# A hybrid attention and mixture-of-experts kernel: numbering of the routing tables on ScalarE, residual sums among the row gathers, and the split of the norm's rows

## The chip, the cores and the metric

The kernel runs on one core of one Trainium2 chip. The metric is the device time of one execution in microseconds (us), the median of several runs. A profiled execution has in addition a span, from its first to its last instruction.

## The reference, cut to what matters

The input x is 16 batches of 256 rows of 128 numbers, 4096 rows in all. Four layers follow one another, each with a layer norm in front and a residual sum behind:

```python
x = x + attn_a(layernorm(x), W_q, W_k, W_v)      # Q, K normalised; one mean vector per batch
x = x + ffn(layernorm(x), ...)                   # first pass of the feed-forward layer
x = x + attn_b(layernorm(x), ...)                # softmax attention, 16 heads of 8
x = x + ffn(layernorm(x), ...)                   # second pass, same weights

def ffn(x, ...):
    router_probs = softmax(x @ gate_w + gate_b)             # 8 experts
    values, indices = top_k(router_probs, k=2)
    values = values / (sum(values) + 1e-9)
    h = gelu(einsum('bsd,edi->bsei', x, ew1) + eb1)
    all_outputs = einsum('bsei,eid->bsed', h, ew2) + eb2
    moe_out = sum over the two chosen experts of value * output
    return x + mlp(x, sh_w1, sh_b1, sh_w2, sh_b2) + moe_out   # mlp: the shared expert
```

So after a feed-forward layer a row holds x + norm(x) + shared expert + two routed experts. The change concerns the norms in front of the first two layers and the first pass of the feed-forward layer, up to its routed part.

## The kernel before, in words

**Engines and order.** Each of the five engines (TensorE = pe, ScalarE = act, VectorE = dve, GpSimd = pool, SyncE = sp) has its own program, written out by hand; semaphores are the only links between them. An engine works strictly in its program's order, so an instruction that waits holds everything that stands behind it. The 4096 rows lie in 32 tiles (T) of 128 rows. Two tiles are a batch or block of 256 rows (NBATCH = NS = 16), eight tiles a group (NG = 4, GT = 8). Numbers that need full precision are held as two float16 halves, high and low.

**The norms** (`norm(r)` on ScalarE at 1452 and on VectorE at 1774, `norm_turns` on TensorE at 939; r = 0 in front of the first layer, r = 1 in front of the second). VectorE makes mean, variance and, with a square root of ScalarE, rstd and shift. Groups 0 and 2 are normalised on VectorE (`norm_rows`, 1793), groups 1 and 3 on ScalarE (`scaled_rows`, 1455). ScalarE then makes the high half of a group (`hi`, 1462), VectorE the low half (`lo`, 1800, line 1803), TensorE transposes the group's batches into four PSUM buffers (line 947), and copies bring them to `xT`: VectorE's for batches 9, 11, 13 and 15, ScalarE's for the others (`copy_out`, 1469). For r = 1 TensorE also makes the gate's logits, batch by batch (`logits`, 951). At r = 0 VectorE, having made its last copy, prepares biases and weights (lines 2497 to 2522) before TensorE may begin the first layer.

**Residual sums** of the second norm (x + norm(x), line 749). GpSimd adds group after group as soon as ScalarE has made that group's high half. `result_shared` on VectorE (2062) adds the shared expert's output to the same tiles and waits for them (`Ln.added`).

**The shared expert** (`up_shared`, `down_shared`; `gelu_shared` on ScalarE). Of the 16 blocks, SA = 12 are done before the routed blocks and 4 behind them. For a block TensorE makes 12 up matmuls, ScalarE 4 Gelus (line 1545), TensorE 16 + 2 down matmuls (lines 1089 and 1092), VectorE one sum (2067). Hidden values and results have two buffers each.

**The inversion of the routing** stands beside these 12 blocks (`route_all` and `invert` on VectorE, `inverse_beside_shared` on TensorE at 1105). VectorE picks the two experts of each row; TensorE counts ranks (`rank`, 1046) behind down product 1; VectorE then computes a slot for each row and expert, sorted by expert. To find which row a slot holds, it compares block and row numbers with columns, for four tiles (a table g of 8) at a time: `oneblk` (128 x 4 x 2 x 78, line 2137) and `onerow` (128 x 4 x 2 x 128, line 2139), two buffers of each. GpSimd multiplies `oneblk` with the rows' numbers (line 758), and TensorE multiplies the two into one bank, `IDX` (`number`, 1096, 8 small matmuls per table). One table stands behind each of the down products 4 to 11. After the last, VectorE makes the row numbers `tok_i` (2155) and `weigh_all` (2194) the eight small steps of the weights `wtop`.

**The routed blocks** (39 blocks of 256 slots). GpSimd gathers each block's rows from memory with two indirect DMAs (`fetch_rows`, 764, line 769) into four buffers; fetch f waits for the turn of block f - 4. For each block TensorE turns the rows (`turn`, line 1166), ScalarE copies them (1571), TensorE makes the up product, ScalarE the Gelu, VectorE splits it into two halves (`split`, lines 2123 and 2125), TensorE makes 24 down matmuls (line 1074), and VectorE writes the result (2183). The loop handles four blocks per turn of the loop (`LOOPED` = 9), each with its expert's number read into registers first. Behind the routed blocks come the last 4 shared blocks, then the combination and the attention.

## Time and profile before

| | |
|---|---|
| median of 3 runs | 814.87 us (811.92 to 815.82) |
| the profiled execution, its own time | 809.36 us |
| its span | 807.5 us |
| mean granted TensorE clock | 0.931 of 2.4 GHz |
| TensorE, weight loads, VectorE, ScalarE, GpSimd busy | 82%, 59%, 78%, 65%, 61% |
| the second norm up to the last logits | 84 to 105 us |
| the shared blocks beside the inversion | 105 to 149 us |
| the routed blocks | 157 to 280 us |

In a profile, PE is TensorE, PEld its weight loads, DVE VectorE, ACT ScalarE, POOL GpSimd, SP SyncE; "L1803" is line 1803 of the kernel. A timeline row gives start, duration, engine, line, operation, output and inputs, number of instructions merged into it, and in brackets the idle time of the engine before it with what ended that. In the chain of waits each piece was released by the one above it. "PEclk" is the share of 2.4 GHz that was granted. All times are counted from the start of the span.

### The profile page before, as it was taken

The page shows a single profiled execution, that of the slowest core. Times are in us where ns is not written, and L with a number is a line of the kernel's source. Part 1 is how long each engine was busy: PE and PEld are TensorE (multiplying, and loading weights), DVE is VectorE, ACT ScalarE, POOL GpSimd, SP SyncE. Part 2 cuts the span into 40 slices and gives each one's busy share as a digit, 9 for nine tenths or more (in the row PEclk, how much of TensorE's full clock was granted, in tenths as well). Part 3 has the DMA queues.
Part 4 walks back from the last instruction along what each step waited for, and adds up shares of the span by engine and source line. Part 5 has one row for each costly group of instructions (what it writes and reads, how often), then busy time and mean ns, then how long its engine had stood idle before and what let it go on. Part 6 is the DMA issues. An engine that isn't in the chain of part 4 may idle for free.

```text
span 807.5 us, 22799 instructions
## 1 busy us (share of the span) xinstructions
PE 660.6 (82%) x7807; PEld 476.5 (59%) x7808; DVE 626.6 (78%) x1404; ACT 523.9 (65%) x1255; POOL 496.0 (61%) x512
## 2 busy tenths in 40 slices
PE   0666399699999946898988899889978989999980
PEld 0343389588988943343433444443447978898870
DVE  6589979477777637999999899999855277878848
ACT  4666764276666634687888788878865556666640
POOL 4997516677887068678248828107877727777730
PEclk9999589799999976699999999999989999999995
DMA  7232210133335411101000100000111323323236
GB/s 206 66 92 33 78 29 1 27 82 89 83 89 78 63 43 39 25 11 41 6 2 15 41 2 1 2 2 16 47 57 53 113 63 84 89 80 87 71 110 208
DMA packets 52505, 46.88 MB, mean 58 GB/s; under 512 B 8771, under 2 KB 44779, under 8 KB 52440
## 3 DMA queue, kind: packets, MB, share of 16 engines
q1 hardware_dynamic: 43352, 28.02, 12.4%
q0 software_dynamic: 9088, 17.98, 9.1%
q8 instruction: 42, 0.69, 0.4%
q14 instruction: 23, 0.19, 0.1%
HBM read 26.76 MB, written 20.13 MB: 58 GB/s over the span
## 4 chain that ended last, share of the span: by engine, by line
PE 48%; DVE 24%; POOL 10%; ACT 8%; issue 7%; DMA 2%; SPq 1%; DVEq 0%; ACTq 0%; POOLq 0%
PE ps L930 23%; PE ps L1074 13%; DVE mx L2371 9%; POOL rows L868 7%; PE ps L1089 3%; PE ps L1325 3%; PE ps L1166 2%; DVE xres L2249 2%; ACT xn L1458 2%; ACT scratch L1665 1%; DVE hlo L2364 1%; DVE hhi L2358 1%; DVE stats L1767 1%; ACT hl L1467 1%; DVE rnorm L1821 1%
## 5 line engine op out<-in xcount | busy, mean ns | idle before, releaser
L1545 ACT ACTIVATE h<-ps,b1T 128x256 f32<-128x256 f32 x440 | 172.1, 480 | 56.6 <-PE ps L930 56.6
L2371 DVE TENSOR_REDUCE mx<-ps 128x2 f32<-128x512 f32 x256 | 171.4, 684 | 16.0 <-PE ps L930 14.9
L1665 ACT ACTIVATE scratch<-ps 128x512 f32<-128x512 f32 x256 | 152.4, 613 | 36.0 <-PE ps L930 34.6
L930 PE MATMUL ps<-xg,w1s 128*128 128x256 f16 x936 | 117.4, 276 | 11.1 <-issue 9.5
L1074 PE MATMUL ps<-w2s,hhi 128*128 x1248 | 117.2, 219 | 0.0
L879 POOL DMA_INDIRECT ytok<-yst,didx x78 | 89.4, 1146 | 42.4 <-DVE yst L2183 21.4
L930 PE MATMUL ps<-kst,qst 32*128 32x256 f16 x512 | 98.1, 286 | 17.1 <-DVE mx L2371 13.5
L769 POOL DMA_INDIRECT scratch<-rows,tok_i x78 | 90.3, 1157 | 26.8 <-issue 23.2
L930 PEld LDWEIGHTS ps<-xg,w1s 128*128 x936 | 88.5, 99 | 25.1 <-issue 14.8
L1571 ACT ACTIVATE xg<-ps 128x512 f16<-128x512 f16 x78 | 46.6, 598 | 83.2 <-PE ps L1166 83.1
L2125 DVE SCALAR_TENSOR_TENSOR hlo<-h,hhi 128x1024 f16<-128x1024 f32 x78 | 95.6, 1226 | 2.7
L930 PE MATMUL ps<-hlo,kst 32*128 32x256 f16 x512 | 94.5, 281 | 1.9 <-ACT scratch L1665 1.8
L1074 PEld LDWEIGHTS ps<-w2s,hhi 128*128 128x128 f16 x1248 | 86.3, 98 | 0.1
L783 POOL DMA_INDIRECT gy<-ysorted,slot_i x64 | 61.8, 966 | 39.5 <-DMA ysorted<-yst 20.2
L1074 PE MATMUL ps<-w2s,hlo 128*128 x624 | 85.7, 219 | 0.0
L1325 PE MATMUL ps<-scratch,vx 128*32 128x256 f32 x1024 | 84.2, 402 | 1.5 <-ACT h L1670 0.7
L868 POOL DMA_INDIRECT rows<-hl,slot_i x64 | 63.4, 991 | 19.9 <-issue 18.8
L930 PEld LDWEIGHTS ps<-kst,qst 32*128 32x128 f16 x512 | 29.8, 93 | 74.8 <-DVE mx L2371 48.5
L2123 DVE TENSOR_SCALAR hhi<-h 128x1024 f16<-128x1024 f32 x78 | 54.4, 698 | 21.0 <-ACT h L1545 17.7
L1089 PE MATMUL ps<-w2f,h 128*128 128x128 f32 x512 | 63.0, 277 | 1.7 <-ACT h L1545 1.6
L2183 DVE SCALAR_TENSOR_TENSOR yst<-ps,b2s 128x256 f32<-128x256 f32 x78 | 33.1, 425 | 37.2 <-PE ps L1074 37.1
L1089 PEld LDWEIGHTS ps<-w2f,h 128*128 128x128 f32 x512 | 59.7, 192 | 2.6 <-ACT h L1545 2.3
(317 smaller groups left out, 1372.6 us busy)
## 6 DMA issues: line engine op xcount, KB each, us to landing
gy<-rows SPq DMA_DIRECT2D x39, 136.0 KB, 2.2
ysorted<-yst SPq DMA_DIRECT2D x39, 128.0 KB, 1.8
h<-in_L_ffn_ew SPq DMA_DIRECT2D x16, 256.0 KB, 3.2
scratch<-ytok SPq DMA_DIRECT2D x16, 256.0 KB, 3.6
xres<-in_L_attn_a_x SPq DMA_DIRECT2D x4, 512.0 KB, 5.6
rows<-hl SPq DMA_DIRECT2D x4, 512.0 KB, 3.1
out_x<-xres SPq DMA_DIRECT2D x4, 512.0 KB, 4.3
scratch<-rows,tok_i POOLq DMA_INDIRECT x78
```

The costliest lines, as they stand in the source:

```text
L769: pool.indirect_dma_start(grow[:, BT * (f % 4) + t, :], None, rows_dram, bass.IndirectOffsetOnAxis(ap=tok_i[:, n:n + 1], axis=0))\
L783: pool.indirect_dma_start(gy[:, f % 4, TOPK * c + k, :], None, y_dram, bass.IndirectOffsetOnAxis(ap=slot_i[:, k, t:t + 1], axis=0))\
L868: pool.indirect_dma_start(region_dram, bass.IndirectOffsetOnAxis(ap=slot_i[:, k, t:t + 1], axis=0), hl[:, t, :], None).then_inc(Post.sent, 16)
L879: pool.indirect_dma_start(ytok_dram, bass.IndirectOffsetOnAxis(ap=didx[:, u, t:t + 1], axis=0), yst[:, u, t, :], None, bounds_check=most, ...
L930: return pe.matmul(o, a, b, start=start, stop=stop)
L1074: last = pe.matmul(YB[u % 2][:, t, :], h[:, u % 2, at:at + P], w, start=(c, k, t) == (0, 0, 0), stop=(c, k, t) == (CH - 1, 2, BT - 1), ski ...
L1089: pe.matmul(YB[q % 2][:, t, :], h32[:, q % 2, at:at + P], w2f[:, c * D:(c + 1) * D], start=(c, t) == (0, 0), stop=False, skip_group_check= ...
L1325: last = pe.matmul(ps[32 * hh:32 * hh + 32, 4, n * SEQ:(n + 1) * SEQ], vx[:, u, kc, 4 * (2 * jp + n) + hh, :], prb[:, (4 * g + hh) % 8, n ...
L1545: last = act.activation(h32[:, u % 2, f], HB[u % 2][:, f], ACT.Gelu_apprx_tanh, bias=b1T[:, ds(e * CH + c, 1)], scale=1.0 / PS)
L1665: act.activation(prb[:, (s // 4 * 4 + (s + 2) % 4) % 8, :], ps[:, s % 2, :], ACT.Exp, scale=HD ** -0.5 / (PS * PS))\
L2125: dve.scalar_tensor_tensor(hlo[:, u, :], h32[:, u, :], XS, hhi[:, u, :], ALU.mult, ALU.subtract)\
L2371: dve.tensor_reduce(mx[:, c, j:j + 5:4], ps[:, 2 + s % 2, :].rearrange("p (n k) -> p n k", n=2), AX_X, ALU.max).then_inc(Att.mx, 1)
```

## The change

It has three parts.

- **Tables.** `oneblk` is multiplied by the rows' numbers on ScalarE, four activations per table (one per tile, the numbers as a per-partition scale), instead of one GpSimd multiplication. On ScalarE table 0 stands before Gelu 4, tables 1 and 2 before Gelu 5, table 3 before 6, 4 and 5 before 7, 6 and 7 before 8. On TensorE two tables stand between each pair of shared products from 3 to 8, the index is complete before down product 7, `rank` stands behind down product 0 instead of 1, and the turns of the first two gathered blocks stand in front of down product 11. VectorE's sums stand one place later in its program.
- **Residual sums.** GpSimd's four sums move from the second norm to behind the gathers of blocks 8, 14, 20 and 26, and wait for the 12 shared results; those no longer wait for the sums, only the last four do.
- **Rows of both norms.** VectorE normalises groups 0, 1 and 3 (24 tiles), ScalarE group 2 (8 tiles), with high and low halves put between them as they come ready.

`bdone` becomes a view of `onerow` (used in the second pass only). The diff, cut to its core:

```diff
@@ gpsimd
-            pool.tensor_copy(ids16[:, :], ids_i[:, :])
+            pool.tensor_copy(ids_c[:, :], ids_i[:, :])
...
-                for g in range(NG):
-                    pool.wait_ge(l.hi, NG + g + 1)
-                    pool.tensor_tensor(group(xres, g), group(xres, g), group(xn, g), ALU.add).then_inc(l.added, 1)
...
-                with pool.Fori(0, T // 8) as i:
-                    for u in range(2):
-                        g = 2 * i + u
-                        pool.wait_ge(m.inblk, g + 1)
-                        ids = ids16[:, ds(4 * g, 4)].unsqueeze(2).unsqueeze(2).to_broadcast([P, 4, TOPK, NT])
-                        pool.tensor_tensor(oneblk[:, u, :, :, :], oneblk[:, u, :, :, :], ids, ALU.mult)\
-                            .then_inc(m.numbered, 1)
...
                 for f in range(NBLK):
                     fetch_rows(f)
+                    if f in (8, 14, 20, 26):
+                        g = (f - 8) // 6
+                        pool.wait_ge(m.y, 2 + SA)
+                        pool.tensor_tensor(group(xres, g), group(xres, g), group(xn, g), ALU.add).then_inc(l.added, 1)
@@ tensor
                 def inverse_beside_shared():
                     up_shared(0)
                     up_shared(1)
-                    for n in range(SA):
+                    down_shared(0)
+                    rank()
+                    mm(IDX, zero16[:, :], zero16[:, 0:NT], True, False)
+                    for n in range(1, SA):
+                        if n + 1 < SA:
+                            up_shared(n + 1)
+                        if 4 <= n < 8:
+                            number(2 * n - 7, 1)
+                        if n == 7:
+                            mm(IDX, zero16[:, :], zero16[:, 0:NT], False, True).then_inc(m.index, 1)
+                        if n == SA - 1:
+                            turn(0, 0, 0)
+                            turn(1, 1, 0)
                         down_shared(n)
-                        if n == 1:
-                            rank()
-                            mm(IDX, zero16[:, :], zero16[:, 0:NT], True, False)
-                        if 4 <= n < 4 + T // 4:
-                            number(n - 4, n % 2)
-                        if n + 2 < SA:
-                            up_shared(n + 2)
-                    mm(IDX, zero16[:, :], zero16[:, 0:NT], False, True).then_inc(m.index, 1)
+                        if 3 <= n < 7:
+                            number(2 * n - 6, 0)
@@ scalar, norm
-                scaled_rows(1)
+                middle = 2 * GT + GT // 2
+                scaled_rows(range(2 * GT, middle))
                 hi(0)
+                scaled_rows(range(middle, 3 * GT)).then_inc(l.by_act, 1)
                 hi(1)
-                scaled_rows(3)
-                for g in range(2, NG):
-                    hi(g)
-                    for b in range(GB * (g - 2), GB * (g - 1)):
-                        copy_out(b)
-                for b in SBATCH[2 * GB:]:
+                hi(2)
+                for b in range(GB):
+                    copy_out(b)
+                hi(3)
+                for b in SBATCH[GB:]:
                     copy_out(b)
@@ scalar, first pass
+                def number(g):
+                    act.wait_ge(m.inblk, g + 1)
+                    for c in range(4):
+                        last = act.activation(oneblk[:, g % 2, c, :, :], oneblk[:, g % 2, c, :, :], ACT.Copy,
+                                              scale=ids_c[:, 4 * g + c:4 * g + c + 1])
+                    last.then_inc(m.numbered, 1)
+
+                def inverse_beside_shared():
+                    tables = {4: (0,), 5: (1, 2), 6: (3,), 7: (4, 5), 8: (6, 7)}
+                    for n in range(SA):
+                        for g in tables.get(n, ()):
+                            number(g)
+                        gelu_shared(n)
@@ vector, norm
-                norm_rows(0)
-                norm_rows(2)
-                for g in range(NG):
-                    lo(g)
+                half = GT // 2
+                norm_rows(range(GT)).then_inc(l.norm, 1)
+                norm_rows(range(GT, GT + half))
+                lo(0)
+                norm_rows(range(GT + half, 2 * GT)).then_inc(l.norm, 1)
+                norm_rows(range(3 * GT, 3 * GT + half))
+                lo(1)
+                lo(2)
+                norm_rows(range(3 * GT + half, T)).then_inc(l.norm, 1)
+                lo(3)
@@ vector, first pass
                 def result_shared(n):
                     q = turn_of(n)
-                    dve.wait_ge(Ln.added if r == 0 else Post.added, n // GB + 1)
+                    if r == 1:
+                        dve.wait_ge(Post.added, n // GB + 1)
+                    elif n >= SA:
+                        dve.wait_ge(Ln.added, n // GB + 1)
...
                     result_shared(0)
-                    result_shared(1)
                     dve.wait_ge(m.rank, 1)
...
-                    result_shared(2)
+                    result_shared(1)
...
-                    result_shared(3)
+                    result_shared(2)
                     for g in range(T // 4):
                         onehot(g, g % 2)
-                        if g >= 2:
-                            result_shared(2 + g)
+                        if g % 2:
+                            result_shared(3 + g // 2)
...
-                    for n in range(2 + T // 4, SA):
+                    for n in range(7, SA):
                         result_shared(n)
```

## Rows read from the trace of the kernel before

**Rows 1.** Busy time by windows: start:end, length, PE, PEld, DVE, ACT, POOL, PEclk, DMA.
```profile
118.00:149.00 31.00, 30.41 (x328) 29.13 (x326) 26.57 (x37) 12.73 (x33) 16.32 (x8) 1.00 0.01 2
149.00:157.50 8.50, 1.43 (x15) 0.77 (x12) 3.41 (x11) 0.97 (x2) 5.97 (x6) 0.72 0.15 39
...
164.70:280.00 115.30, 111.01 (x1529) 104.20 (x1526) 89.09 (x114) 78.30 (x192) 78.68 (x67) 1.00 0.39 82
```

**Rows 2.** The chain of waits from 90 to 290 us: start us, us, what.
```profile
153.79 2.65 DMA scratch<-rows,tok_i
...
157.48 2.74 PE ps L930 x12
...
164.70 1.34 PE ps L1074 x24
...
175.24 1.48 PE ps L930 x12
...
187.40 1.48 PE ps L930 x12
```

**Rows 3.** Timeline of 83 to 106 us; last, line 1803 alone (ns min/median/max).
```profile
86.10 4.28 DVE L1795 SCALAR_TENSOR_TENSOR xn<-xres,mean,rstd 128x128 f32<-128x128 f32 x16
...
90.43 13.25 POOL L749 TENSOR_TENSOR xres<-xres,xn 128x1024 f32<-128x1024 f32 x4 [9.78 <-ACT hl L1467]
...
98.09 3.17 ACT L1471 ACTIVATE xT<-ps 128x512 f16<-128x512 f16 x6
...
101.62 0.58 PE L947 MATMUL ps<-ident,hl 128*128 128x128 f16 x4 [0.17 <-DVE hl L1803]
...
L1803 DVE SCALAR_TENSOR_TENSOR hl<-xn,hl x4: 1226/3040/3375, 90.4 to 98.2; 128x1024 f16<-128x1024 f32 x4
```

**Rows 4.** Timeline of 10 to 36 us, the first norm and its end.
```profile
25.47 1.07 ACT L1467 ACTIVATE hl<-xn 128x1024 f16<-128x1024 f32 x1
...
35.10 1.14 PE L930 MATMUL ps<-waT,xT 128*128 128x384 f16 x3 [4.21 <-DVE gws L2521]
```

**Rows 5.** VectorE's timeline from 103 us; then line 2137 alone (ns min/median/max).
```profile
115.05 0.42 DVE L2067 SCALAR_TENSOR_TENSOR xres<-ps,xres 128x256 f32<-128x256 f32 x1 [2.78 <-PE ps L1092]
...
152.65 0.22 DVE L2202 TENSOR_TENSOR wtop<-topp,rs 128x64 f32<-128x64 f32 x1
...
L2137 DVE TENSOR_TENSOR oneblk<-iota,blk x8: 797/1274/1830, 122.3 to 143.4; 128x624 f16<-128x624 f16 x8
```

**Rows 6.** TensorE's timeline from 118 us: up product, down product, up product.
```profile
118.24 1.47 PE L930 MATMUL ps<-xT,w1s 128*128 128x256 f16 x12
119.55 1.95 PE L1089 MATMUL ps<-w2f,h 128*128 128x128 f32 x16
...
121.45 1.47 PE L930 MATMUL ps<-xT,w1s 128*128 128x256 f16 x12
```

**Rows 7.** ScalarE's groups, shapes apart: busy us, mean ns, idle before.
```profile
L1545 ACT ACTIVATE h<-ps,b1T 128x256 f32<-128x256 f32 x440 | 172.1, 480 | 56.6 <-PE ps L930 56.6
...
L1649 ACT ACTIVATE kst<-ps,kxrow 128x512 f16<-128x512 f32 x32 | 22.6, 708 | 5.8 <-PE ps L930 5.8
...
L1458 ACT ACTIVATE xn<-xres,shift,rstd 128x128 f32<-128x128 f32 x32 | 12.7, 488 | 0.6 <-DVE shift L1790 0.6
```

**Rows 8.** The routed loop: gathers, VectorE's split, chain (turn, down), gathers' line.
```profile
165.24 1.24 POOL L769 DMA_INDIRECT scratch<-rows,tok_i  x1 [0.30 <-issue]
...
187.90 1.31 POOL L769 DMA_INDIRECT scratch<-rows,tok_i  x1 [0.31 <-issue]
...
207.00 1.23 DVE L2125 SCALAR_TENSOR_TENSOR hlo<-h,hhi 128x1024 f16<-128x1024 f32 x1
...
185.34 0.22 PE ps L1166 x4
...
209.88 1.34 PE ps L1074 x24
...
L769 POOL DMA_INDIRECT scratch<-rows,tok_i x78: 951/1074/1667, 149.8 to 262.5; - x78
```

57 lines of the change are left out of this document (29 added, 28 removed).

## The prediction

> **What bounds the kernel now.** I read the page first: TensorE is the busiest engine (82% in the table above), so what counts is where it stands still. A table by windows then shows three stretches [rows 1]. From 118 to 149 us TensorE is busy 30.4 of 31 us at full clock (granted 1.00, 2.4 GHz): the shared products beside the inversion of the routing. From 149 to 157.5 us it is busy 1.4 of 8.5 us, and the granted clock falls to 0.72, a mix of the 2.4 and the 1.2 GHz level. From 164.7 to 280 us it is the bound again (111 of 115.3 us). The chain of waits names the hole [rows 2]: the last shared product ends near 149, VectorE writes tok_i, GpSimd issues four gathers 1.26 us apart, the rows land, turn, copy, and the first routed product starts at 157.48; its twelve matmuls take 2.74 us, where the same twelve take 1.48 at 175.24, so that the hole goes on costing after it has ended. The first routed down product starts at 164.70. I use that as the landmark, because behind it TensorE is a steady machine of 12.16 us per four blocks (175.24 to 187.40).
>
> Two more places are touched: the second norm, whose end is held by the residual sums on GpSimd, and the first norm, which ends into a VectorE chain that holds TensorE till 35.10.
>
> **The second norm (84 to 105).** GpSimd's four sums run 90.43 to 103.7 [rows 3]. VectorE's split into high and low (L1803) takes 1.23 us at its shortest and 3.38 at its longest. The starts fit a port that one engine holds for a whole operation: the first split ends at 91.6, the second appears to run only after the first sum (93.76) and ends at 94.90, the last waits for the third sum and ends at 101.49; it follows that a sum holds VectorE for about 3.33 − 1.15 = 2.2 us. TensorE's turn of batch 12 at 101.62 waits for that last split. The page "GPSIMD Engine Reference" of the Trainium skill (Key points) says that GpSimd and VectorE share their SBUF interfaces, with contention for VectorE instructions that have two SBUF inputs or run in a 2-port mode; the trace agrees (1.23 against 3.38 us), and by that rule the sums will hurt again wherever they go.
> With the sums gone and 24 of 32 rows on VectorE at 4.28/16 = 0.27 us against 0.38 on ScalarE (0.49 less an overlap of 0.11 [rows 3, 7]), I laid the new order out: shift ready 86.2; rows 0 to 7 by 88.3; high half 0 till 89.5; low 0 till 90.7; rows 8 to 15 by 91.8; high 1 till 92.9; high 2 till 93.9; low 1 and 2 till 95.4; last rows by 96.5; high 3 till 97.5; low 3 by 98.9. The copies of batches 4 on then start at 97.5 instead of 98.09, and the 0.3 us hole before 101.62 closes. That is 0.9 us; the bounds are 0 (TensorE's own pace of 0.64 us per batch) and 1.5.
>
> **The first norm.** Same reordering, GpSimd still busy splitting weights. High 3 comes at about 24.9 instead of 25.47 and VectorE's chain to 35.10 moves with it [rows 4]: 0.5 us, bounds 0 and 1.
>
> **The products of the tables.** Removed: eight GpSimd multiplications, 16.32/8 = 2.04 us each, which ran beside VectorE's one-hots and stretched the small one-hot from 0.80 to 1.83 us [rows 1, 5]. Added: 32 ScalarE activations of 156 elements with one per-partition operand. None such is in the trace. Nearest: the Gelu, one such operand, 256 elements, 480 ns; L1649, one operand, 512 elements, 708; L1458, two operands, 128 elements, 488 [rows 7]. The slope of the first two is 228/256 = 0.89 ns, so 480 − 100 × 0.89 = 0.39 us each. Four Gelus take 1.57 us in a row, so neighbours overlap by 0.11: a table is 4 × 0.28 + 0.1, about 1.25 to 1.3 us. I take that; the ends are 1.1 and 4 × 0.39 + 0.1 = 1.65 (L1458's own).
> The page "ScalarE: Activation LUTs" of the Trainium skill (What ACT_TABLE_LOAD costs) gives 280 ns + 0.833 ns per element with an overlap of 93 ns, an estimated 1.35 us per table, half a microsecond dearer over all eight.
>
> Moved: the count of ranks goes from behind the second to behind the first shared down product. Before, the scan waits behind result 1, VectorE idle 2.78 us [rows 5]. Now TensorE waits about 0.3 us for the mask, which takes half of the 0.9 us from the norm, but the one-hots start at 118.5 instead of 122.25. Then two tables stand between each pair of shared products. TensorE's work from up product 4 (117.8 instead of 118.24) to the end of the index is five ups of 1.31, four downs of 1.90 [rows 6] and eight numberings of 0.30, 16.6 us, so 134.4 without waits. ScalarE's is eight tables of 1.25 in a row and four Gelus of 1.47, 15.9 us from 119.3, plus the last numbering: 135.6. Neither runs freely: a table must precede its numbering, and the Gelu in front of it waits for the up product. Stepping both engines through the order, TensorE waits 0.85 us before number 1, 0.2 before 3, 0.5 before 4 and 0.7 before 6; the index ends at 136.6. VectorE (1.87 us per one-hot pair, results between) ends at 134.5, its bexp chain at 137.1, and tok_i at 137.3. What is queued behind a waiting table on ScalarE is a Gelu, and for that a down product.
> Then downs 7 to 11, ups 9 to 11 and two turns: 9.5 + 3.9 + 0.5 = 13.9 us, to 150.5. The gathers start at 137.5 and need 6.7 us for the second turn (149.8 to 156.48 [rows 2, 8]); it is asked for at 148: covered by 4 us. Late next is wtop: result 11 at 151.05 and 2.83 us of weights (eight steps after result 11's end at 150.04, the last ending at 152.87 [rows 5]) end at 153.9, just when the first routed Gelu does. With 0.4 us of register loads the first routed product starts at 150.95, at full clock since nothing in front of it idles over 1 us (here the clock fell only in a stretch with 7 us idle [rows 1]). From there to the first routed down: 3 × 1.31 + 2 × 0.22, register loads 0.5, a copy 0.3 = 5.2 us, at 156.15. Against 164.70: **8.6 us**. Each 0.1 us on a table moves that by 1.0 us; the ends are 5.2 and 10.8.
>
> **What goes into the routed loop.** Four sums of 3.33 us among 78 gathers. Three costs. First, GpSimd: gathers take 1.26 us each alone, but beside VectorE eight take 12.17 us, TensorE's own pace, with pieces of 1.31 and 1.67 [rows 8]. From 165.24 to 187.90, sixteen took 22.66 us (1.42 each), so a late GpSimd regains about 0.3 us per block. Fetch 14 starts at 187.90, 2.3 us behind turn 10 (185.56); TensorE needs its rows 12.17 us after that turn, and a block is there 4.1 us after its first gather starts (1.4 to the second, and 2.7 from that to the turn, as from 153.79 to 156.48), so a lag of 8.0 is free. With four sums: 3.5, then 2.3 + 3.4 = 5.7, 4.0 + 3.4 = 7.4, 5.7 + 3.4 = 9.1: about 1 us over at the end, or nothing if it regains faster; I take 0.5. Second, VectorE: each sum holds it 2.2 us. Its low half of a block ends at 208.23 and TensorE wants it at 209.88 [rows 8], 1.65 us of slack, so 0.55 at most per sum, less where the sum meets idle time: I take 0.4 × 4 = 1.5. Third, the wait for all twelve results (y ≥ 14) in front of the first sum: met at 151, asked at about 160, nothing. The results of the last four batches wait for the sums; these end by 240, asked near 270, nothing. Together 2.0 us, ends 0 and 16.4 (below).
>
> **Sum.** 8.6 + 0.5 − 2.0 = 7.1 us (the 0.9 of the second norm is inside the 8.6). The profiled execution took 809.36 us, span 807.5: forecast 802.3. It lies 5.5 below the median of the runs, 814.87; against that, **807.8**.
>
> **Rivals.**
> 1. *The loop pays.* If GpSimd never regains (the trace's steady 12.17 us per eight gathers is exactly TensorE's pace), the lag is 2.3 + 13.3 = 15.6 against 8.0 free: 7.6 us of wait for rows, after the third and fourth sum; and if VectorE's slack does not help, 4 × 2.2 = 8.8. Together 16.4 − 9.1: **822.2**. It decides from a loop cost of 9.1 us. For: the locked pace. Against: 1.42 us per gather while it was behind, and 1.65 us of slack.
> 2. *ScalarE becomes the bound beside the shared products*: tables of 1.65 us or more plus semaphore hops of 0.1 at each of eight hand-overs take 3.5 + 0.8 from the gain: 7.1 − 4.3 = 2.8, **812.1**. For: L1458's 488 ns and the zero slack of the order. Against: L1458 has an operand more.
> 3. *Nothing is handed back*: loop free, norms at their better ends (+1.1), tables at 1.2 (+1.0): gain 11.2, **803.7**.
>
> **How the numbers follow.** A measurement of this kernel can tell from no change about 0.5%, 4.1 us. Forecast 0.62 (of it 0.04 within 0.5%); rival 1 0.10 (0.07 slower, 0.03 same, for it can be paid in part); rival 2 0.14 (0.11 same, 0.03 faster); rival 3 0.10, faster; the rest 0.04, mostly same or slower. Faster 0.72, same 0.19, slower 0.09. The range goes from a gain of 12.4 (rival 3 and a microsecond of scatter) to none: 802.5 to 815.0; it leaves out rival 1 and a little on either side.
>
> **What would show each step.** Right: TensorE without an idle stretch over 1 us between 118 and 160 and a granted clock of 1.00 there; tok_i near 137; the table activations near 400 ns; L1803 near 1.23 us in the second norm and the gate product ending near 104.3; four L749-like sums in the loop with VectorE's L2125 once stretched by each, and TensorE idle under 1 us beside each. Wrong: TensorE waiting for gathered rows after the third sum; activations near 490 ns and TensorE idle over 1 us before several numberings; the loop's pitch over 12.2 us; or a first routed product later than 154.

## The result, and the profile after

The kernel after the change takes 817.65 us (median of 20 runs, 809.46 to 822.40), the kernel before 811.56 us (20 runs, 806.95 to 816.12): ratio 1.0056, 95% interval 1.0034 to 1.0077. A ratio leaves out the executions that ran over 1.5% above the fastest of their kernel, so it need not be the quotient of the two medians beside it. By the ratio the change is slower by 4.5 us (the medians are 6.1 apart), outside my range and on the side to which I had given 0.09. The profiled execution of after took 817.84 us, span 816.0, mean granted clock 0.93.

First, one table of landmarks, read from the timelines of both profiled executions (start times in us): the first layer's first product; the second norm's shift; the first step of the routing; tok_i; the first and the last routed down product.

| | first layer | shift | routing | tok_i | first down | last down | span |
|---|---|---|---|---|---|---|---|
| before | 35.1 | 86.0 | 105.2 | 149.2 | 164.5 | 280.2 | 807.5 |
| after | 42.9 | 91.7 | 109.7 | 143.0 | 162.3 | 284.7 | 816.0 |

So the first norm loses 7.8 us (2.1 come back inside the first layer), the middle from shift to first down gains 7.9 (78.5 to 70.6), and the routed loop loses 6.7 (115.7 to 122.4): 4.5 us late at the last routed down product, as much as the ratio shows. That the two agree to a tenth is luck: behind this point the execution loses 4.0 us more, in code that the change leaves alone except for `bdone`. The stretch behind it lay between 527.1 and 532.8 us in six executions of six kernels, and between 527.1 and 531.3 in three that don't differ there (late_split, n0_old, after), so I take it for scatter; landmarks say nothing about the whole to better than some 3 us.

**The middle, as forecast.** Windows of after (start:end, length, PE, PEld, DVE, ACT, POOL, PEclk, DMA), which answer to [rows 1]; then its chain of waits, which answers to [rows 2].

```profile
118.00:143.00 25.00, 22.74 (x249) 21.12 (x248) 22.66 (x40) 19.66 (x57) 0.00 (x0) 1.00 0.00 1
143.00:156.80 13.80, 13.80 (x135) 13.36 (x135) 1.94 (x5) 7.08 (x18) 9.33 (x10) 1.00 0.16 42
162.30:284.70 122.40, 112.47 (x1535) 104.22 (x1533) 95.68 (x114) 78.37 (x191) 88.46 (x69) 1.00 0.34 76
```

```profile
155.00 1.84 PE ps L1084 x16
156.96 1.32 PE ps L925 x12
158.84 1.01 ACT h L1548 x3
159.94 0.60 ACT xg L1574
160.76 1.48 PE ps L925 x12
162.46 1.34 PE ps L1069 x24
```

The hole is gone: TensorE is busy 13.80 of the 13.8 us behind tok_i at full clock, the gathers lie under the last shared products, and the first routed product comes straight behind them. The third window holds the loss: TensorE is busy hardly longer than before (112.5 us; 111.4 in the loop of before), but stretched over 122.4 us instead of 115.7.

**The first norm.** VectorE's timeline of after; below it line 1811 (VectorE's rows) alone, then the same work in the kernel before. Min/median/max in ns.

```profile
13.10 3.23 DVE L1811 SCALAR_TENSOR_TENSOR xn<-xres,mean,rstd 128x128 f32<-128x128 f32 x12
17.36 2.02 DVE L1819 SCALAR_TENSOR_TENSOR hl<-xn,hl 128x1024 f16<-128x1024 f32 x1 [1.03 <-ACT hl L1469]
19.30 6.59 DVE L1811 SCALAR_TENSOR_TENSOR xn<-xres,mean,rstd 128x128 f32<-128x128 f32 x8
25.82 3.71 DVE L1819 SCALAR_TENSOR_TENSOR hl<-xn,hl 128x1024 f16<-128x1024 f32 x2
29.46 3.94 DVE L1811 SCALAR_TENSOR_TENSOR xn<-xres,mean,rstd 128x128 f32<-128x128 f32 x4
```

```profile
L1811 DVE SCALAR_TENSOR_TENSOR xn<-xres,mean,rstd x24: 337/348/1235, 13.1 to 32.7; 128x128 f32<-128x128 f32 x24
```

```profile
L1795 DVE SCALAR_TENSOR_TENSOR xn<-xres,mean,rstd x16: 342/343/346, 13.1 to 17.1; 128x128 f32<-128x128 f32 x16
```

A "row" here is one instruction, for one tile of 128 rows. Twelve of them cost 0.27 us each, the next eight 0.82 on average, the last four 0.99. GpSimd begins to split the weights at 16.3 us, and that is where the price changes. In the kernel before, VectorE's 16 were done by 17.4: thirteen stood ahead of GpSimd's start at 16.43, and the last three kept their price. The averages hide the pattern. For five rows from 20.80 on, GpSimd's instructions and VectorE's rows alternate one to one: each row starts just behind a GpSimd instruction and ends about 0.15 us behind that instruction's end. The first two of each, GpSimd's timeline, then VectorE's:

```profile
20.65 1.23 POOL L724 TENSOR_TENSOR w1s<-h,w1s 128x512 f32 x1 [0.18 <-POOL w2s L722]
21.85 1.20 POOL L726 TENSOR_TENSOR w2s<-h,w2s 128x512 f32 x1
```

```profile
20.80 1.23 DVE L1811 SCALAR_TENSOR_TENSOR xn<-xres,mean,rstd 128x128 f32<-128x128 f32 x1
21.95 1.23 DVE L1811 SCALAR_TENSOR_TENSOR xn<-xres,mean,rstd 128x128 f32<-128x128 f32 x1
```

ScalarE then waits for rows, and TensorE for the end of VectorE's chain, which answers to [rows 4]: ScalarE's timeline, then TensorE's.

```profile
22.07 2.00 ACT L1469 ACTIVATE hl<-xn 128x1024 f16<-128x1024 f32 x2 [3.21 <-DVE xn L1811]
...
33.43 1.06 ACT L1469 ACTIVATE hl<-xn 128x1024 f16<-128x1024 f32 x1 [7.42 <-DVE xn L1811]
```

```profile
42.93 1.46 PE L925 MATMUL ps<-waT,xT 128*128 128x384 f16 x4 [4.07 <-DVE gws L2545]
```

**The second norm** has no such partner any more. Its low halves all take 1.23 us (the maximum in [rows 3] was 3.38), and from shift to routing it takes 18.0 us instead of 19.2.

```profile
L1819 DVE SCALAR_TENSOR_TENSOR hl<-xn,hl x4: 1218/1226/1227, 95.1 to 103.1; 128x1024 f16<-128x1024 f32 x4
```

**The routed loop.** What TensorE waits for in it, after, then before: us in total, times, longest.

```profile
PE ps L925 <- issue: 3.2, 6, 0.6
PE ps L925 <- ACT h L1548: 2.7, 3, 1.0
PE ps L1109 <- DMA scratch<-rows,tok_i: 2.1, 3, 1.0
PE ps L1069 <- DVE hlo L2149: 1.8, 2, 1.2
```

```profile
PE ps L930 <- issue: 4.2, 8, 0.6
```

Before, the loop had register loads ("issue") and nothing else. Now there are 6.6 us of waits for rows, for VectorE's low halves and for Gelus, and 1.0 us less in front of register loads; with 1.1 us more of busy time that is the 6.7. Of the three Gelu waits one follows a wait for rows (222.4 us) and one a wait for a low half (236.0); the third (251.0) follows neither. Of the waits for rows one (1.05 us at 222.4) comes behind the third sum; the last (0.90 us at 274.5) is a transfer that took 6.3 us from its issue to the turn, not a gather issued late. The chain of after shows how a sum acts: gathers, the sum of 2.36 us, and gathers again with no gap between them. VectorE's timeline shows the split of the same block: the high half takes 3.44 us instead of 0.69. The four sums take 2.62, 2.36, 2.36 and 2.37 us, and the high halves beside them 1.85, 3.44, 2.84 and 2.85.

```profile
188.53 0.95 POOL scratch L760
189.51 2.36 POOL xres L770
192.03 1.24 POOL scratch L760
193.27 0.30 issue
193.57 1.17 POOL scratch L760
```

```profile
188.45 0.42 DVE L2207 SCALAR_TENSOR_TENSOR yst<-ps,b2s 128x256 f32<-128x256 f32 x1 [1.05 <-PE ps L1069]
188.99 3.44 DVE L2147 TENSOR_SCALAR hhi<-h 128x1024 f16<-128x1024 f32 x1
192.46 1.22 DVE L2149 SCALAR_TENSOR_TENSOR hlo<-h,hhi 128x1024 f16<-128x1024 f32 x1
```

### The profile page after: what moved, and what is told of

The parts are those of the page before. It is cut to its first block, busy times and chain, and to the rows that moved or that the text cites. A ratio compares the mean times of both kernels' runs of the same rounds, so it can differ in the third digit from the quotient of the medians.

```text
span 816.0 us, 22788 instructions
## 1 busy us (share of the span) xinstructions
PE 662.5 (81%) x7807; PEld 475.7 (58%) x7808; DVE 635.7 (78%) x1420; ACT 527.5 (65%) x1271; POOL 476.9 (58%) x504
## 4 chain that ended last, share of the span: by engine, by line
PE 38%; DVE 27%; POOL 15%; issue 8%; ACT 7%; DMA 3%; SPq 1%; ACTq 0%; DVEq 0%; POOLq 0%
PE ps L925 19%; DVE mx L2395 10%; PE ps L1069 9%; POOL rows L863 7%; POOL scratch L760 5%; PE ps L1084 2%; PE ps L1327 2%; DVE xres L2273 2%; DVE xn L1811 2%; PE ps L1109 2%; DVE hlo L2388 1%; DMA scratch<-rows,tok_i 1%; ACT scratch L1681 1%; ACT h L1548 1%; DVE hl L1819 1%
## 5 line engine op out<-in xcount | busy, mean ns | idle before, releaser
L760 POOL DMA_INDIRECT scratch<-rows,tok_i x78 | 92.4, 1184 | 90.0 <-DVE tok_i L2179 66.0
L1069 PEld LDWEIGHTS ps<-w2s,hhi 128*128 128x128 f16 x1248 | 86.2, 98 | 2.3 <-issue 2.1
L2147 DVE TENSOR_SCALAR hhi<-h 128x1024 f16<-128x1024 f32 x78 | 62.3, 799 | 11.2 <-ACT h L1548 7.9
```

What stands on the lines that cost most here:

```text
L760: pool.indirect_dma_start(grow[:, BT * (f % 4) + t, :], None, rows_dram, bass.IndirectOffsetOnAxis(ap=tok_i[:, n:n + 1], axis=0))\
L1069: last = pe.matmul(YB[u % 2][:, t, :], h[:, u % 2, at:at + P], w, start=(c, k, t) == (0, 0, 0), stop=(c, k, t) == (CH - 1, 2, BT - 1), ski ...
L2147: dve.tensor_scalar(hhi[:, u, :], h32[:, u, :], XS, None, ALU.mult).then_inc(m.hi, 1)
```

## The experiments

All are edits of the kernel after. Two theories for the loop stood against each other: **hold** (GpSimd's sum keeps VectorE out, and the down product waits for its low half) and **late gathers** (the sum pushes GpSimd back, and the turn waits for rows). The first four runs shared a chip with before at 809.92 us. All later ones, the kernel before included, ran on chips on which every execution took some 14% longer (before 922 to 943 us); they have ratios to before on their own chip, and landmarks that scatter by several us: the loops with neither a sum nor an extra gather in them took 123.5 to 128.6 us there in six executions, against 115.6 in both on the first chip. The kernel before was not profiled on these chips.

**1. First norm in the old order** (n0_old): for r = 0 alone, 16 rows on each engine and the halves behind them; everything else as after. VectorE's part of the edit:

```diff
+        OLD, BY, NO = (True, False), (0, 3), (0, 2)
...
+                if OLD[r]:
+                    norm_rows(range(GT)).then_inc(l.norm, 1)
+                    norm_rows(range(2 * GT, 3 * GT)).then_inc(l.norm, 1)
+                    for g in range(NG):
+                        lo(g)
```

> The changed kernel with the first norm alone in its old order (16 rows on VectorE, 16 on ScalarE); all else changed. Theory A (a port: each of VectorE's short two-input row operations waits out a weight-splitting operation of GpSimd, and 24 rows pay more of that than 16): the first layer starts at about 35.1 us instead of 42.9, the second norm's shift is made at 86.0 instead of 91.7, and the end comes 5 to 6 us earlier than the changed kernel's, median ratio to the kernel before about 1.000 (0.997 to 1.003). Rival (the first layer gives the delay back in full, or the loss lies in the routed loop alone): the ratio stays at 1.005 or more although the first layer starts earlier.

Measured: 811.56 us (12 runs), ratio 1.0003 (0.9977 to 1.0028). The first layer is back near its old place (35.9 us), shift at 85.7, tok_i at 136.4, first down at 155.7; the loop still takes 121.7. The first norm cost the change about 0.5% of the time, and the rest of it is neutral: a gain in the middle that the loop gives back. (At the last down product this execution is still 2.8 us ahead of before, 277.4 against 280.2; the ratio doesn't show it.) Its waits in the loop:

```profile
PE ps L926 <- issue: 3.2, 6, 0.6
PE ps L926 <- ACT h L1566: 2.8, 3, 1.0
PE ps L1070 <- DVE hlo L2175: 1.8, 2, 1.2
PE ps L1110 <- DMA scratch<-rows,tok_i: 1.4, 2, 1.0
```

On a chip of the second kind (n0_old_2):

> The kernel of n0_old again (four sums between the gathers, tables and second norm as changed), on the same chip as late_gathers: 6 us longer in the loop than n0_old_dve_sums, 121.7 us, or 131 us where everything takes 14% longer; ratio to before 0.998 to 1.003 or, on the latter chip, 0.992 to 1.000.

Measured: 924.64 us (12 runs), ratio 1.0006 (0.9961 to 1.0050); loop 132.5 us, a little over the expected 131; the wait for rows is gone, the others are still there: 2.7 us for low halves and 3.5 for Gelus.

**2. The weights split later** (late_split): the change as it is, but GpSimd waits for the first norm.

```diff
+            pool.wait_ge(Ln.lo, NG)
             with pool.Fori(0, E // 2) as i:
```

> The changed kernel, but GpSimd begins to split the experts' weights only after the first norm's last low half, so nothing runs on GpSimd beside the norm's rows. Theory A: VectorE's row operations take 0.34 us each throughout (none above 0.5), and the first layer starts at about 34.5 us, before the old 35.1; whether the end gains depends on when the splitting, begun some 10 us later, ends (it may then hold the second stage). Rival (the rows are slow for VectorE's own reasons, such as the order with the low halves between): rows stay at 0.8 us and the first layer starts at 42.9.

Measured: 808.74 us (10 runs), ratio 0.9972 (0.9948 to 0.9995), which is 0.84% or 6.8 us under after's 1.0056. TensorE begins the first layer at 33.6 us, earlier than in any other kernel here. All 24 rows keep their price. Take GpSimd away and the same order of rows costs nothing: that settles the first norm. The first layer then takes longer (to shift 86.8), so that of the 9.3 us by which it starts earlier than after, 4.9 are left. VectorE's rows, and TensorE's timeline:

```profile
L1812 DVE SCALAR_TENSOR_TENSOR xn<-xres,mean,rstd x24: 343/345/349, 13.1 to 23.9; 128x128 f32<-128x128 f32 x24
33.60 2.74 PE L926 MATMUL ps<-waT,xT 128*128 128x384 f16 x8 [4.09 <-DVE gws L2546]
```

**3. The sums back in the second norm** (sums_back), the rest as after.

```diff
+                for g in range(NG):
+                    pool.wait_ge(l.hi, NG + g + 1)
+                    pool.tensor_tensor(group(xres, g), group(xres, g), group(xn, g), ALU.add).then_inc(l.added, 1)
...
-                    if f in (8, 14, 20, 26):
-                        g = (f - 8) // 6
```

> The changed kernel with GpSimd's four residual sums back in the second norm, the 12 shared results waiting for them again; all else changed. Theory B (four sums among the gathers cost the routed loop 6.7 us, partly by holding VectorE's high half 2.7 us, partly by making the gathers late): first to last routed down product 115.7 us instead of 122.4, no wait of TensorE for gathered rows or for the low half inside the loop; the second norm is longer by about 1.3 us; net 4 to 6 us earlier than the changed kernel, ratio about 0.999 to 1.001. Rival (the loop is slower because its gathers started earlier and fell into another phase with VectorE): the loop stays above 120 us without any sum in it.

Measured: 819.29 us (6 runs), ratio 1.0092 (1.0057 to 1.0128). The loop is at 115.6 us again, so its whole loss is the sums'. The ratio that I expected (0.999 to 1.001) did not come: the second norm takes 24.3 us instead of 18.0, where I had expected little over a microsecond, because VectorE's longer work now meets the sums. Two rows take 2.43 and 2.42 us instead of 0.34, and two low halves 4.52 together.

```profile
96.52 4.27 DVE L1810 SCALAR_TENSOR_TENSOR xn<-xres,mean,rstd 128x128 f32<-128x128 f32 x8
100.86 4.52 DVE L1818 SCALAR_TENSOR_TENSOR hl<-xn,hl 128x1024 f16<-128x1024 f32 x2
100.91 6.67 POOL L750 TENSOR_TENSOR xres<-xres,xn 128x1024 f32<-128x1024 f32 x2 [2.10 <-ACT hl L1468]
108.55 1.06 ACT L1468 ACTIVATE hl<-xn 128x1024 f16<-128x1024 f32 x1 [4.82 <-DVE xn L1810]
```

**4. The sums on VectorE** (n0_old_dve_sums): the first norm old, no sum on GpSimd, one of them behind each of the shared results 7 to 10, where VectorE sits idle for 2.78 us in front of each next result in the profile of after.

```diff
                     for n in range(7, SA):
                         result_shared(n)
+                        if n < SA - 1:
+                            g = (2, 3, 0, 1)[n - 7]
+                            dve.wait_ge(m.y, 2 + n + 1)
+                            dve.tensor_tensor(group(xres, g), group(xres, g), group(xn, g), ALU.add)\
+                                .then_inc(Ln.added, 1)
```

> First norm in its old order, and the four residual sums on VectorE (one behind each of the shared results 7 to 10, where VectorE idles more than half of the time and GpSimd only issues gathers). Theories A and B together: first layer from 35.1, loop 115.7 us, the changed kernel's gain of 8 us between the second norm and the routed blocks kept whole: ratio to the kernel before about 0.990 (0.987 to 0.994). Rival (VectorE, loaded with 4 x 1.2 us, is late with the weights and with the first routed split): first routed down product over 1.5 us later after the shift than in the changed kernel (70.8 us), ratio above 0.995.

Measured: 803.75 us (6 runs), ratio 0.9899 (0.9864 to 0.9934): it beats both kernels. Loop 115.6 us, first down 156.0, last 271.6. The sums take 1.23 us each and delay nothing; its loop has no wait but "issue".

```profile
L2207 DVE TENSOR_TENSOR xres<-xres,xn x4: 1224/1225/1226, 139.1 to 148.8; 128x1024 f32<-128x1024 f32 x4
```

Again on the second kind of chip (n0_old_dve_sums_2):

> The kernel of n0_old_dve_sums again, on the same chip as the three above, so that they have a reference: ratio to before 0.987 to 0.993, loop 115.6 us.

Measured: 927.43 us (6 runs), ratio 0.9867 (0.9806 to 0.9929); loop 125.3 us. The loops below are set against the ones without a sum from the same chip.

**5. Sums behind the last gather** (sums_last): n0_old, with the four sums moved out of the loop of gathers. No gather can be late; VectorE is still held.

```diff
                     fetch_rows(f)
-                    if f in (8, 14, 20, 26):
-                        g = (f - 8) // 6
...
+                for g in range(NG):
+                    pool.wait_ge(m.y, 2 + SA)
+                    pool.tensor_tensor(group(xres, g), group(xres, g), group(xn, g), ALU.add).then_inc(l.added, 1)
```

> First norm as before, second norm as changed, and GpSimd's four sums moved from between the gathers of blocks 8 to 26 to behind the last gather. No gather can then come late; VectorE is still held by each sum, in the last four blocks or in the shared blocks behind them. Against n0_old (four sums between the gathers, loop from first to last routed down product 121.7 us) and n0_old_dve_sums (none, 115.6 us). Theory A, the late gathers cost the 6.1 us: the loop is 115.6 to 116.5 us and the whole is 5 us under n0_old, ratio to before about 0.993 to 0.995. Theory B, holding VectorE costs them, 1.5 us a sum: the loop is near 119 to 121 us (the sums that fall within the last four blocks), ratio about 0.999. One point against A even if the loop is short: the first shared block behind the loop waits for the sums, up to 3 us, to be seen in front of the last four shared blocks.

Measured: 938.72 us (10 runs), ratio 0.9994 (0.9951 to 1.0038), where n0_old_dve_sums_2 beside it has 0.9867. Loop 130.9 us, 4.5 and 5.6 over the two loops without a sum on the same chip (126.4 and 125.3), with the sums in its last blocks. VectorE's timeline, then TensorE's:

```profile
277.13 2.52 DVE L2172 TENSOR_SCALAR hhi<-h 128x1024 f16<-128x1024 f32 x1
279.68 3.25 DVE L2174 SCALAR_TENSOR_TENSOR hlo<-h,hhi 128x1024 f16<-128x1024 f32 x1
```

```profile
277.00 0.27 PE L1069 MATMUL ps<-w2s,hhi 128*128 x2 [0.80 <-DVE hlo L2174]
...
283.06 0.27 PE L1069 MATMUL ps<-w2s,hhi 128*128 x2 [3.02 <-DVE hlo L2174]
```

Holding VectorE is enough to lose the gain, with 3.8 us in two waits for the low half; late gathers aren't needed. But here the sums follow one another and hold low halves, while in the change they stand apart and hold high halves, with 1.8 us of waits for the low half. So this run shows that the hold alone can cost as much; how the 6.1 us divide in the change itself stays open.

**6. One sum left** (one_sum, three times): n0_old_dve_sums with the sum of group 0 on GpSimd, behind the gathers of block 14.

```diff
+                    if f == 14:
+                        pool.wait_ge(m.y, 2 + SA)
+                        pool.tensor_tensor(group(xres, 0), group(xres, 0), group(xn, 0), ALU.add).then_inc(l.added, 1)
```

> First norm old; three of the four sums on VectorE beside the shared products, the fourth on GpSimd behind the gathers of block 14. Theory B1 (costs are cumulative: each sum makes GpSimd about 2.7 us later, it never regains that while VectorE works, and only a lateness of more than 8 us reaches TensorE): one sum costs at most the 1.4 us of one hold of VectorE's split, no wait of TensorE for gathered rows; first to last routed down 115.6 to 117.1 us. Theory B2 (each sum costs its own share, 6.5/4 = 1.6 us): 117.2 with a wait of its own for rows or split each time.

> As one_sum (there the loop was 126.9 us with and without the one sum). B1 (costs cumulative): 115.6 to 117.1 us from first to last routed down, no wait for rows. B2 (each sum costs its own share): 117.2.

> One sum (group 0) on GpSimd in front of gather 14, the other three on VectorE. If the loss is one lump per sum (VectorE held, or gathers late for a stretch that ends) the loop is 115.6 + 1.5 = about 117.1 us. If the first sum already uses up GpSimd's lead and only the later ones cost, it is 115.6 to 116.2. If GpSimd's lead once lost stays lost to the end, so that every fourth register read waits for rows, it is 118 or more.

Measured: 917.21 us, ratio 0.9912 (0.9856 to 0.9968); 925.16 us in 4 runs, beside 922.76 for before, too few for an interval; 932.45 us, ratio 0.9902 (0.9858 to 0.9947). Loops 126.9, 125.8 and 127.1 us. Each of the three shows exactly one wait of TensorE for a low half (0.5, 1.0 and 1.1 us), and none for rows. In the loop as a whole a single sum doesn't stand out from the scatter:

| chip | loops without a sum, us | loops with |
|---|---|---|
| of one_sum | 126.9 (tables_only), 128.6 (pool_tables) | one sum 126.9; eight halves 133.0 |
| of one_sum_2 | 123.5 (tables_only_2), 127.4 (pool_tables_2) | one sum 125.8; eight halves 132.4 |
| of one_sum_3 | 125.3 (n0_old_dve_sums_2), 126.4 (norms_old_dve_sums) | one sum 127.1; sums_last 130.9 |
| of n0_old_2 | none | four sums 132.5; late_gathers 142.6 |

So whether one sum costs its quarter of the 6.1 us, or less, is not settled.

**7. Eight half sums** (halves, twice): n0_old, with a sum of four tiles behind the gathers of every third block from 8 on.

```diff
-                    if f in (8, 14, 20, 26):
+                    if f in range(8, 32, 3):
+                        half = ds(GT // 2 * ((f - 8) // 3), GT // 2)
```

> First norm old; the four sums of 8 tiles in the loop cut into eight of 4 tiles, behind the gathers of blocks 8, 11, 14 ... 29. Theory: a half sum holds VectorE for about 1.2 us, less than its slack of 1.65, so TensorE's waits for the low half (1.8 us in the changed kernel) vanish; the lateness of the gathers stays, since the total is the same or larger: waits for rows 2 to 4 us; first to last routed down 118 to 120.5 us instead of 121.7. Rival (the waits come from the number of interruptions, not from their length): 123 us or more.

> As halves (there the loop was 133.0 us against 126.9 without sums, so 6.1 us for the eight halves). Length theory: 118 to 120.5 us, waits for rows remain, waits for the low half vanish. Rival (lateness of GpSimd alone decides, and it depends on the total time on GpSimd): 121 us or more, nearly all as waits for rows, even with no wait for the low half.

Measured: 926.28 us, ratio 0.9959 (0.9886 to 1.0031), loop 133.0; 926.86 us, ratio 1.0028 (0.9955 to 1.0101), loop 132.4. I had expected 118 to 120.5 us for the first chip, some 2 us under whole sums; they are no better than whole sums (132.5). Half of that theory came: TensorE waits for low halves 0.8 us in one run and not at all in the other. But it waits 4.3 and 4.6 us for Gelus. A half sum takes 1.3 to 1.5 us and still holds a high half for up to 1.8 (2.45 instead of 0.69).

**8. More gathers instead of sums** (late_gathers): n0_old_dve_sums with two extra gathers of 128 rows, into a tensor that nobody reads, in front of the gathers of blocks 8, 14, 20 and 26 (the sums stood behind them).

```diff
+                    if f in (8, 14, 20, 26):
+                        for t in range(BT):
+                            pool.indirect_dma_start(spare[:, (f - 8) // 3 + t, :], None, rows_dram,
+                                                    bass.IndirectOffsetOnAxis(ap=tok_i[:, BT * f + t:BT * f + t + 1], axis=0))\
+                                .then_inc(gate_split, 16)
                     fetch_rows(f)
```

> n0_old_dve_sums (no sum on GpSimd, loop 115.6 us where the chip is as for the first runs, 125 to 126 us where everything takes 14% longer) with two more gathers of 128 rows each, into a tensor of their own that nobody reads, at each of the four places in front of gathers 8, 14, 20 and 26 where the change has its sums: some 2.5 us of GpSimd each time, as long as a sum, but nothing that holds VectorE for long. Theory A, the gathers that then come late cost the loop its time: the loop is 4 to 7 us longer than without, and TensorE waits for rows. Theory B, holding VectorE is what costs: the loop is within 1.5 us of the one without, ratio to before 0.987 to 0.992, even if the gathers behind such a place run late.

Measured: 930.52 us (12 runs), ratio 1.0067 (1.0030 to 1.0103), so no faster than with the sums (1.0006 beside it, with an interval that overlaps); loop 142.6 us. Neither theory had that. Its profiled execution took 937.06 us, 6.5 us over its median, so the loop's figures hold for that execution alone. VectorE's halves are not held (every low half in the loop takes 1.22 to 1.25 us), and TensorE has no wait for rows. GpSimd is not behind either: it waits for TensorE's turns, 24.6 us in all. TensorE's waits are put down to "issue" and to the copy of turned rows, and its clock falls in the loop, where n0_old_2 has 1.00 in the same two windows. VectorE waits 28.8 us in front of the routed results for an event that the trace doesn't name (11.1 in n0_old_2); by the kernel's order it waits there for its result buffer to be written out (`m.y_out`). TensorE's waits, VectorE's, then two windows:

```profile
PE ps L930 <- issue: 9.5, 11, 2.1
PE ps L1074 <- issue: 6.3, 14, 1.0
PE ps L930 <- ACT xg L1596: 2.7, 2, 2.0
DVE yst L2242 <- remote: 28.8, 12, 4.4
```

```profile
180.00:200.00 20.00, 17.08 (x189) 14.70 (x187) 11.52 (x15) 10.27 (x25) 12.67 (x12) 0.83 0.35 68
200.00:220.00 20.00, 16.38 (x199) 14.87 (x198) 11.57 (x15) 10.27 (x25) 12.97 (x13) 0.91 0.24 69
```

What stopped TensorE there the trace doesn't name (matmul records are missing beside several of these waits). The run was meant to price late gathers and doesn't: they never became late. What late gathers cost by themselves stays open.

**9. The parts of the middle.** tables_only (twice) has both norms old and the sums back in the second norm, so that of the change only the tables and the order of the products are left. norms_old_dve_sums has both norms old and the sums on VectorE. pool_tables (twice) is n0_old_dve_sums with GpSimd multiplying the tables again, in the new order of the products:

```diff
+                for g in range(T // 4):
+                    pool.wait_ge(m.inblk, g + 1)
...
-                        for g in tables.get(n, ()):
-                            number(g)
                         gelu_shared(n)
```

> Both norms in their old order and the four sums back in the second norm; of the change only the part with the tables is left (numbering on ScalarE, two tables between shared products, ranks one product earlier, turns before the last shared down). Theory (the three parts are separable): first layer from 35 to 36 us as before, shift to routing 19.2 us as before, routing to first routed down product 52.6 us instead of 59.3, loop 115.7; so the end 6.7 us earlier, ratio about 0.992 (0.989 to 0.996). Rival (the stage gained only because GpSimd and VectorE were relieved by the other parts): routing to first routed down product above 55 us.

> The same kernel as tables_only, whose call met a chip on which every execution, the kernel before included, took 14% longer with idle time at TensorE put down to issue. Same expectations: shift to routing 19.2 us, routing to first routed down 52.6 us, first to last routed down 115.7, ratio 0.989 to 0.996.

> Both norms as before (16 rows to 16 each), tables and their products as changed, the four sums on VectorE between the last shared results. Against n0_old_dve_sums, which differs only in the second norm's split: shift to first route step was 19.2 us with the old split and 17.4 to 18.0 with 24 to 8. If the 24 to 8 split of the second norm is worth what those profiles say, this one is 1.2 to 1.8 us slower than n0_old_dve_sums, ratio to before 0.991 to 0.993. If the old split without GpSimd's sums beside its low halves is as short as the new one (17.5 us), the two are equal, at 0.990.

> The version with the first norm old and the sums on VectorE, but the tables multiplied on GpSimd again (one operation each), in the new order of two tables between shared products. Theory C (ScalarE is what lets two tables stand between products; on GpSimd each small one-hot of VectorE waits for the running multiplication and takes 1.8 us instead of 0.8): VectorE needs about 2.9 us per table instead of 1.9, tok_i at about 142 instead of 136.7, TensorE waits 4 to 6 us more before the numberings; routing to first routed down 56 to 58 us instead of 52.6. Rival (the order alone gives the gain; ScalarE was nearly the bound and is now relieved): 51 to 53 us.

> As pool_tables (there tok_i came at 142.3 against 138.0, and the small one-hots were slowed). Theory C: tok_i near 142, routing to first routed down 56 us or more. Rival, by the slow chip's numbers (the delay is hidden by the time in which the gathers wait for their turn anyway): tok_i near 142, but routing to first routed down 53 to 54 us.

| | us | ratio to before | shift to routing | routing to first down |
|---|---|---|---|---|
| tables_only | 916.76 | 0.9862 (0.9816 to 0.9908) | 19.2 | 56.4 |
| tables_only_2 | 914.97 | 0.9928 (0.9881 to 0.9975) | 19.2 | 57.4 |
| norms_old_dve_sums | 928.23 | 0.9867 (0.9806 to 0.9929) | 18.9 | 57.4 |
| n0_old_dve_sums_2 | 927.43 | 0.9867 (0.9806 to 0.9929) | 17.4 | 56.0 |
| pool_tables | 921.27 | 0.9888 (0.9813 to 0.9962) | 18.1 | 57.3 |
| pool_tables_2 | 920.54 | 1.0027 (0.9974 to 1.0081) | 17.5 | 57.3 |

The tables and their order carry the gain: with both norms as before the ratio is 0.986 to 0.993, and tables_only, which leaves the sums where the kernel before has them, is not behind the versions with the sums on VectorE. (From routing to first down it takes 56.4 and 57.4 us where I expected 52.6; every kernel but late_gathers takes some 56 to 58 us on these chips.) The second norm's 24 to 8 split is 1.5 us in the landmarks and nothing that the runs can tell. With the tables on GpSimd, tok_i comes 38.6 us behind the routing instead of 33.3, and the first routed up product 51.8 us behind it instead of 48.6 to 49.2, yet the first routed down is no later: something else holds it in the other kernels on these chips, and I didn't find out what. The two ratios disagree (0.9888, which rests on three of ten executions, and 1.0027), and what ScalarE's part is worth apart from the order stays open.

## Why the prediction was wrong, point by point

- **The middle: right.** Counted from shift, I had tok_i at 51.1 us (137.3 − 86.2) and the first routed product at 64.75; measured 51.3 and 65.1. A table took 1.37 us on ScalarE from its first start to its last end (407 to 438 ns an activation); I had 1.25 to 1.3. The estimate of 1.35 by the Trainium skill's page "ScalarE: Activation LUTs" (What ACT_TABLE_LOAD costs) was nearer. TensorE waited three times in front of a numbering, 2.3 us in all, as stepped. Gathers covered, clock 1.00, weights just in time: also as stepped. From shift to first down 7.9 us against 8.6, the second norm 1.2 against 0.9.
- **The first norm: the wrong sign, −0.5 forecast and +7.8 measured at its end.** The step that failed is "same reordering, GpSimd still busy splitting weights". I priced VectorE's rows at 4.28/16 us, a row from the second norm before its sums began, and gave bounds of 0 and 1. Of the first norm's own rows in the kernel before, thirteen of sixteen stood ahead of GpSimd's start and the last three just at it, and the change put twelve of 24 behind it, where they cost 0.82 to 0.99. I had argued that very exclusion from [rows 3] for the second norm and not asked whether it held here. The Trainium skill's page "GPSIMD Engine Reference" (Key points) names such instructions (two SBUF inputs), and the trace agrees, 0.27 against 0.82 us.
- **The loop: the mechanism right, the size wrong, 2.0 us forecast and 6.7 measured.** Term by term. *The hold of VectorE* was to be 2.2 us a sum and to cost 1.5: the high halves were held 1.2, 2.8, 2.2 and 2.2 us, 2.05 on average, and TensorE waited 1.8 us for low halves, so this term stands. *Late Gelus* had no term at all: 2.7 us of waits, 1.7 net of the register loads that they replace. *Late rows* were to cost 0.5: 2.1 measured, of which 0.9 is the one slow transfer. The other 1.1 us is longer busy time. The lag of the gathers behind the turns came out near the forecast, by luck: at most 9.3 us against 9.1 (gathers of block 29 behind turn 25), since a sum took 2.4 to 2.6 us of GpSimd instead of 3.33, and GpSimd regained less than 0.3 us per block (from 192.03 to 210.09 twelve gathers took 1.50 us each, as long as TensorE's own pace; against that pace even the 1.42 of [rows 8] is 0.2 us per block). Nor does the lag decide, as "a lag of 8.0 is free" has it: block 22 had a lag of 8.0 and came 1.05 us late, because its gathers were stretched to 1.89 and 1.67 us and its rows were there 5.7 us behind the first gather's start (216.59 to 222.33), not 4.1; block 29 had 9.3 and was in time.
- **The rivals.** Rival 1, *the loop pays*, had the side and the premise (nothing is regained), at 0.10. Its 16.4 us were more than twice too many, and at the measured 6.7 us it would not have made the change slower: 8.6 + 0.5 − 6.7 leaves a gain of 2.4. The side turned on the first norm, for which I had no rival. Rivals 2 and 3 didn't come.
- **By the parts**: +7.8 − 2.1 (first norm, less what the first layer returns) − 7.9 (middle) + 6.7 (loop) = +4.5 us. Undo the first norm and it is level (1.0003); take the sums off GpSimd too and it is 0.9899, 8.2 us, near the 8.6 of the middle with nothing taken back.

## What to carry to other kernels

The duration of a VectorE instruction in a trace holds for what GpSimd was doing at that moment. Before more such work is put into a stretch, look at when GpSimd's work starts and ends there, and price by a row that has the same neighbour. A large elementwise sum is not cheap just because it stands on an engine that isn't the bound: four of 2.4 us on GpSimd cost 6.1 us of the loop (121.7 against 115.6), and the same sums on VectorE, in idle gaps of 2.8 us, took 1.23 each and cost nothing. Look whether an engine has any reserve before counting on it to catch up: in the loop before, GpSimd waited for TensorE's turns 0.3 us in all, and otherwise worked without a pause until its last gather.

## What the runs showed of the hardware that I had not expected

- A VectorE instruction with one input (high half of 128 x 1024) was held by a GpSimd sum too, 3.44 us instead of 0.69. I had counted on it for the low half (L2125), with its two inputs, alone. The high half runs at 0.67 ns per element where the low half takes 1.20, and the sentence on the shared interfaces in my prediction names a 2-port mode beside the two inputs; that this is that mode no run shows.
- A VectorE instruction that meets one of GpSimd's pays by the length of GpSimd's, not by its own. A row of 128 elements took 1.12 to 1.23 us beside weight-splitting instructions of 1.08 to 1.23 us, and 2.43 beside a sum of 3.4 us (sums_back); the high half of 1024 took 1.85 to 3.44 us beside sums of 2.4 to 2.6, and 2.1 to 2.45 beside half sums of 1.3 to 1.5. So a chain of small VectorE instructions loses most, if GpSimd has a stream of its own. It fits a turn-taking by whole instructions; the traces show the starts and ends, not what does the locking.
- Eight extra gathers into an unread tensor cost about 2% of the whole (1.0067 against 0.9867 for the same kernel without them, each to before on its own chip). In the profiled execution VectorE waits longer for its result buffers and TensorE's granted clock falls to 0.83 in one window; why is open.
